# First attention of a decoder layer: rotated queries, scores over 64 rows, the mask as a TensorE product

## The chip, the core and the metric

The kernel runs on one core of one Trainium2 chip. The metric is the device time of one execution in microseconds. Three timed runs of the kernel before gave 1333.85, 1334.43 and 1336.25 us, so its median is 1334.43 us.

## The reference, cut to what matters

The program is one pre-norm decoder layer on x of shape (16, 128, 256): `x += attn(ln(x))`, `x += xattn(ln(x), ctx)`, `x += ffn(ln(x))`. Only the first attention is changed. It has 16 query heads, 4 key heads, a head size of 128 and a window of 64:

```python
q, k = rope((x @ Wq).heads(16)), rope((x @ Wk).heads(4))   # t * cos + rotate_half(t) * sin
v = (x @ Wv).heads(4)
s1 = q[..., :64] @ k[..., :64].T / 8                       # two score maps for each head
s2 = q[..., 64:] @ k[..., 64:].T / 8
s1, s2 = where(allowed, s1, -1e30), where(allowed, s2, -1e30)
a1, a2 = softmax(s1), softmax(s2)
d = relu(a1 - lam * a2);  d = d / (d.sum(-1) + 1e-6)
out = (d @ v).merge() @ Wo
```

`rotate_half` exchanges the two halves of 64 features, with a minus on one of them. So a rotated query needs, for each row, a value that stands 64 rows away.

## The kernel before, in words

One program, with instructions put by hand on five in-order queues: TensorE (PE), VectorE (DVE), ScalarE (ACT), GpSimd (POOL) and SyncE (SP, which issues the DMAs). Semaphores join them. Three stages follow one another: first attention (to about 500 us), cross attention (to about 890 us), the feed-forward part with its experts.

In the first attention the outer loop runs over 4 groups of heads (one key head and its 4 query heads), and in each group over 16 units `u`, one per sequence of the batch. So there are 64 units, n = 16g + u. Four units make a chunk; j = u mod 4 is the place in it. Features stand on the 128 partitions, tokens on the free axis. While the units of one chunk are worked on, the projections of the next chunk are made beside them: six items, k, q0 to q3 and v, each over 4 x 128 tokens. `A_SLOT` (L288) says at which place (j, slot) each item is made; slot 0 is at the beginning of a unit, slot 1 behind the transposes. `A_ITEMS` (L286) is their order. All go through one PSUM bank (PJ), so TensorE starts an item only when the one before has been taken out of the bank (`a_pf` for k and q, `a_vf` for v).

What the engines do for a unit, each in its own order (`a_unit` of each engine):

- TensorE: slot 0; the scores of unit n (L669); transposes of the weights of unit n-2 (L683, L685), which wait for POOL's norm; slot 1; the product with v (L692), which waits for ACT's copy `pt`; the output projection of unit n-3 (L701). Slot items are L553 (k, q) and L608 (v).
- DVE: denominator and its reciprocal for n-2 (L1100, L1105); the addition to x (L1110); `rec` and `ratio` for n-1 (L1080, L1084), which wait for the exponentials of n-1; the take of the slot 0 item (`a_take`); `rho` (L1088); `oal` (L1140); the difference of the two maps of n-1 (`a_diff`, L1094, 4 instructions); the maxima of the scores of n (L1148, L1149); the take of the slot 1 item.
- ACT: slot 0 (v is taken by ACT); the copy `pt` for n-2; the clipping of unit n-1 (L1500, 4 times with its sum), which waits for DVE's difference; the 8 exponentials of unit n (L1456), which wait for the maxima; the copy `oah`; and last the mask (L1511), copied into the two PSUM banks that the scores of unit n+2 will add onto.
- POOL: the norm of unit n-2 (L1687, 2 instructions) behind `rden`; the addition that finishes the rotated key (`a_keys`, L1681); at some units low parts of weights.

The rotation before is asymmetric. The key is rotated in full: DVE writes k\*cos and the crossed k\*sin into `ktmp` (3 instructions), POOL adds them, and SP copies the result with 4 DMAs into `kva`, so that map m has its 64 key rows twice (L462 to L465). The query is not rotated: DVE writes two products of it with tables (`qab`, L1054), and the score product contracts over 128 rows, which adds up both terms of the rotation. A score product takes 64 queries (stationary) against 128 or 64 keys; heads of odd and even number go to the upper and lower 64 PSUM partitions.

The start differs: the first chunk's items go through four banks (`turns` = 4), and the two first units put the mask under the scores by a product of the identity with `maskb` (L665).

Of the kernel before, what the change touches and what calls it, by code (L numbers as in the profile page):

```python
# [106 lines left out]
def decoder_kernel(nc, x, ctx_in, in_wqk, in_wv, in_wo, in_lam, in_taba, in_rawb, in_tabb, in_kvtab,  # L107
# [11 lines left out]
    with ctx:  # L119
# [129 lines left out]
        a_kd, a_tn = sem("a_k_copied"), sem("a_table_negated")  # L249
        a_sc, a_mx, a_ex = sem("a_scores"), sem("a_negmax"), sem("a_exp")  # L250
        a_mk = sem("a_mask_in_place")
# [34 lines left out]
        A_ITEMS = ["k", "q0", "q1", "q2", "v", "q3"]  # L286
        AN, AV = len(A_ITEMS), A_ITEMS.index("v")
        A_SLOT = {(0, 1): 0, (1, 0): 1, (1, 1): 2, (2, 1): 3, (3, 0): 4, (3, 1): 5}  # L288
# [152 lines left out]
        def _(sp):  # L441
            for c in range(NC):
# [6 lines left out]
                if c == 1:  # L449
                    sp.dma_start(taba[:, :, :], in_taba).then_inc(a_tab, 16)  # L450
# [6 lines left out]
            for g in range(NG):  # L457
                if g < NG - 1:
                    sp.wait_ge(a_lo, g * AW + AW)
                    sp.dma_start(raw_a[:, :, :], in_wqk[g + 1]).then_inc(a_raw, 16)  # L460
                for c in range(NC):
                    sp.wait_ge(a_k, g * NC + c + 1)  # L462
                    for m in range(2):
                        for at in (0, 64):
                            sp.dma_start(kva[at:at + 64, c % 2, m, :], ktmp[64 * m:64 * m + 64, 0, :]).then_inc(a_kd, 16)  # L465
# [81 lines left out]
        def _(pe):  # L547
# [69 lines left out]
            def a_unit(g, u, first=False, final=False, drain=False):  # L617
# [286 lines left out]
            pe.wait_ge(a_vf, 1)  # L904
            pe.wait_ge(s_cst, 3)
# [81 lines left out]
        def _(dve):  # L987
# [47 lines left out]
            def a_take(g_to, c, item, turns=1):  # L1035
# [6 lines left out]
                if item == 0:  # L1042
                    wait(dve, a_kd, 64 * chunk)
# [916 lines left out]
```

## Time and profile before

| | before |
|---|---|
| median of 3 runs | 1334.43 us |
| profiled execution | 1336.08 us, its span 1334.2 us |
| TensorE busy | 1262.3 us (95%) |
| VectorE busy | 837.2 us (63%) |
| ScalarE busy | 720.2 us (54%) |
| GpSimd busy | 467.6 us (35%) |
| granted TensorE clock, mean | 0.986 |

The span is what the engines' records cover; the execution's own time is 1.9 us longer. PE counts a matmul from issue to its modelled end, and PEld, its weight load, runs beside it. A matmul in fp32 leaves two records, so the 16 score products of a unit show as x32. "Idle before" behind a row says how long the engine stood before the instruction and what released it. A line number can be that of a helper: ACT's copies all stand at L1423 and go by their tiles, `ps<-maskb` being the mask.

### The profile page before, as it was taken

What the parts mean: (1) busy time and instruction counts of PE and PEld (TensorE: products, weight loads), DVE (VectorE), ACT (ScalarE), POOL (GpSimd) and SP (SyncE); (2) the same over time, 40 slices, a digit from 0 to 9 for tenths busy, and PEclk for the clock granted to TensorE, in tenths of its full rate; (3) what the DMA queues carried; (4) which work ended last, traced back from release to release, by engine and by line L of the source; (5) the groups of instructions that cost most, each with busy time, mean ns of one, the idle gap of its engine ahead of it and who ended that gap; (6) DMA issues with size and microseconds to landing.
All of it is one profiled execution on the core that took longest, in us unless ns stands there. A gap on an engine that the chain in (4) does not pass through costs nothing.

```text
span 1334.2 us, 27286 instructions
## 1 busy us (share of the span) xinstructions
PE 1262.3 (95%) x9584; PEld 993.9 (74%) x9584; DVE 837.2 (63%) x1986; ACT 720.2 (54%) x2746; POOL 467.6 (35%) x451
## 2 busy tenths in 40 slices
PE   5799999999999787999999999989999999999998
PEld 4678888888887564666666666657888888888887
DVE  6788888888888676566666656775443443434433
ACT  2788888888887753444444444464232332423322
POOL 3122113212211124445444544641152353533532
PEclk9899999999999989999999999999899999999999
DMA  6002000200012101111202101200324341144340
GB/s 222 17 18 57 18 17 18 57 17 17 17 34 92 31 16 48 60 33 58 67 17 92 33 17 33 76 1 1 111 67 139 68 126 52 39 139 77 57 93 31
DMA packets 34737, 72.78 MB, mean 55 GB/s; under 512 B 7872, under 2 KB 12992, under 8 KB 33344
## 3 DMA queue, kind: packets, MB, share of 16 engines
q1 hardware_dynamic: 34624, 71.32, 20.2%
q8 instruction: 66, 1.08, 0.3%
q14 instruction: 47, 0.39, 0.1%
HBM read 52.29 MB, written 2.23 MB: 41 GB/s over the span
## 4 chain that ended last, share of the span: by engine, by line
PE 74%; DVE 9%; ACT 8%; issue 4%; POOL 2%; DMA 1%; SPq 1%; DVEq 0%; POOLq 0%; ACTq 0%
PE ps L553 33%; PE ps L945 9%; PE ps L669 5%; PE ps L701 4%; PE ps L738 3%; PE ps L832 3%; ACT ea L1456 3%; PE ps L692 3%; PE ps L842 2%; PE ps L814 2%; PE ps L822 2%; PE ps L608 2%; ACT ea L1500 2%; DVE ea L1094 1%; PE ps L683 1%
## 5 line engine op out<-in xcount | busy, mean ns | idle before, releaser
L1828 POOL TENSOR_TENSOR sg<-sg,cw 128x512 f32<-128x512 f32 x88 | 113.6, 1291 | 260.4 <-ACT sg L1619 257.0
L1397 DVE TENSOR_TENSOR hh<-ps,sg 128x512 f32<-128x512 f32 x100 | 69.1, 691 | 179.1 <-POOL sg L1828 161.4
L1423 ACT ACTIVATE hhh<-hh 128x512 fp32r<-128x512 f32 x100 | 63.2, 632 | 213.8 <-DVE hh L1397 211.6
L1456 ACT ACTIVATE ea<-ps,negmax 128x64 f32<-128x64 f32 (+1 forms) x512 | 165.1, 342 | 6.7 <-DVE negmax L1149 6.7
L1423 ACT ACTIVATE pt<-ps 128x512 f32<-128x512 f32 x128 | 77.1, 602 | 169.7 <-PE ps L822 112.2
L1196 DVE TENSOR_TENSOR qcs<-ps,tabb 128x512 f32<-128x512 f32 x192 | 123.5, 686 | 64.8 <-PE ps L553 64.4
L553 PE MATMUL ps<-xnh,wch 128*128 128x512 f32 x400 | 157.3, 393 | 0.0
L553 PE MATMUL ps<-xnl,wch 128*128 128x512 f32 x400 | 157.1, 393 | 0.0
L553 PE MATMUL ps<-xnh,wcl 128*128 128x512 f32 x400 | 155.7, 389 | 0.0
L1687 POOL TENSOR_TENSOR ea<-ea,rden 128x128 f32<-128x128 f32 (+1 forms) x128 | 62.2, 506 | 263.1 <-DVE rden L1105 263.1
L1694 POOL TENSOR_TENSOR eb<-eb,rsum 128x512 f32<-128x512 f32 x64 | 67.4, 1054 | 180.2 <-DVE rsum L1240 180.0
L945 PE MATMUL ps<-wch,hhh 128*128 128x256 f32 x400 | 115.8, 290 | 4.2 <-DVE hhl L1399 2.4
L1399 DVE TENSOR_TENSOR hhl<-hh,hhh 128x512 fp32r<-128x512 f32 x100 | 75.5, 755 | 69.8 <-ACT hhh L1423 69.8
L945 PE MATMUL ps<-wch,hhl 128*128 128x256 f32 x400 | 113.6, 284 | 0.0
L945 PE MATMUL ps<-wcl,hhh 128*128 128x256 f32 x400 | 113.6, 284 | 0.0
L1456 ACT ACTIVATION_READ_ACCUMULATOR ea<-ps,negmax 128x1 f32 x512 | 107.3, 210 | 0.0
L1456 ACT ACTIVATE eb<-ps,negmax 128x128 f32<-128x128 f32 x256 | 90.7, 369 | 26.0 <-DVE negmax L1234 25.7
L669 PEld LDWEIGHTS ps<-kva,qab 128*64 128x64 f32 x2048 | 93.8, 140 | 13.2 <-issue 8.1
L669 PE MATMUL ps<-kva,qab 128*64 128x128 f32 (+1 forms) x2048 | 103.0, 254 | 0.0
L1619 ACT ACTIVATE sg<-ps 128x512 f32<-128x512 f32 x100 | 59.8, 598 | 71.9 <-PE ps L553 71.2
L701 PE MATMUL ps<-woh,oah 128*128 128x256 f32 x256 | 97.5, 381 | 0.7 <-DVE oal L1140 0.7
L1054 DVE TENSOR_TENSOR qab<-ps,taba 128x512 f32<-128x512 f32 x128 | 82.1, 683 | 19.5 <-PE ps L553 19.0
(154 smaller groups left out, 3307.3 us busy)
## 6 DMA issues: line engine op xcount, KB each, us to landing
raw_w<-in_rawb_dram SPq DMA_DIRECT2D x4, 2432.0 KB, 8.9
kva<-ktmp SPq DMA_DIRECT2D x64, 128.0 KB, 2.3
kvt<-qcs SPq DMA_DIRECT2D x64, 128.0 KB, 2.3
cw<-comb_d SPq DMA_DIRECT2D x32, 256.0 KB, 5.0
raw_w<-in_rawc_dram SPq DMA_DIRECT2D x4, 1920.0 KB, 8.4
cw<-comb_d SPq DMA_DIRECT2D x16, 224.0 KB, 4.8
raw_a<-in_wqk_dram SPq DMA_DIRECT2D x4, 768.0 KB, 5.8
cw<-comb_d SPq DMA_DIRECT2D x16, 192.0 KB, 5.8
```

The source lines that it names most:

```text
L553: last = pe.matmul(out_ap, w, m, start=n == 0, stop=n == len(steps) - 1)
L669: last = pe.matmul(to[rows, h // 2, :], qab[:, c % 2, m, h, S * j + at:S * j + at + QH], kva[:, c % 2, m, S * j:S * j + keys], start=False ...
L701: last = pe.matmul(ps[:, YB, 0:DM], o_[:, (u - 3) % 2, h, :], w_[:, h, :], start=h == 0 and i == 0, stop=h == HG - 1 and i == 2)
L945: last = pe.matmul(ps[:, j // 2, DM * (j % 2):DM * (j % 2 + 1)], h_[:, par, S * j:S * (j + 1)], w_[:, t, 2 * KT * 128:RC_T], start=begin a ...
L1054: last = dve.tensor_tensor(quads(dst), src, bcast(taba[:, tab, :]), ALU.mult)
L1196: last = dve.tensor_tensor(quads(qcs[:, b_at(t), m, :]), quads(bk), bcast(tabb[:, b_table(t), m, :]), ALU.mult)
L1397: dve.tensor_tensor(hh[:, par, :], bank(C_U[par]), sg[:, par, :], ALU.mult).then_inc(c_h, 1)
L1399: dve.tensor_tensor(hhl[:, par, :], hh[:, par, :], hhh[:, par, :].bitcast(f32), ALU.subtract)\
L1423: return act.activation(dst, src, ACT.Copy)
L1456: last = act.activation(dst(m, h), src, ACT.Exp, bias=negmax[:, par, i:i + 1], accum_out=sums[:, par, i:i + 1])
L1694: pool.tensor_tensor(src[:, par, :, :], src[:, par, :, :], rec[:, par, :].unsqueeze(2).broadcast_to([128, HG, S]), ALU.mult).then_inc(done, 1)
L1828: pool.tensor_tensor(sg[:, par, :], sg[:, par, :], cw[:, c % 2, t, :], ALU.mult).then_inc(c_hs, 1)
```

## The change

The query is now rotated too. DVE writes q\*cos into `qab[:, par, 0, h]` and q\*sin into `qab[:, par, 1, h]`; two DMAs for each head carry the latter, its halves exchanged, into the place of the other parity; POOL adds the two. The key goes from POOL's addition straight into `kva`, with no copy. Each score product contracts over the 64 rows of its own map, so the two maps use different halves of the array's rows, and the order alternates over the four quarters. The mask goes under the scores of every unit as two products of the identity with `maskb`, and ACT's copy of it is gone; the scores of unit n wait for the exponentials of unit n-2 instead. The items move to other slots, and v becomes the last.

```diff
-        A_ITEMS = ["k", "q0", "q1", "q2", "v", "q3"]
+        A_ITEMS = ["k", "q0", "q1", "q2", "q3", "v"]
-        A_SLOT = {(0, 1): 0, (1, 0): 1, (1, 1): 2, (2, 1): 3, (3, 0): 4, (3, 1): 5}
+        A_SLOT = {(0, 0): 0, (0, 1): 1, (1, 0): 2, (1, 1): 3, (2, 0): 4, (3, 0): 5}
...
@@ SP, for each chunk @@
-                    sp.wait_ge(a_k, g * NC + c + 1)
-                    for m in range(2):
-                        for at in (0, 64):
-                            sp.dma_start(kva[at:at + 64, c % 2, m, :], ktmp[64 * m:64 * m + 64, 0, :]).then_inc(a_kd, 16)
+                    for h in range(HG if g or c else 0):
+                        sp.wait_ge(a_pf, (g * NC + c) * AW + (h + 2))
+                        for to, at in ((64, 0), (0, 64)):
+                            sp.dma_start(qab[to:to + 64, 1 - c % 2, 1, h, :], qab[at:at + 64, c % 2, 1, h, :])\
+                              .then_inc(a_qx[h], 16)
@@ TensorE, a_unit @@
-                        pe.wait_ge(a_kd, 64 * (g * NC + (c + 1)))
-                    wait(pe, a_mk, n - 1)
+                        pe.wait_ge(a_k, g * NC + (c + 1))
+                        pe.wait_ge(a_qr, HG * (g * NC + (c + 1)))
+                    wait(pe, a_ex, n - 1)
                     for m in range(2):
-                        sc = A_S[u % 2][:, m, 0:SW]
-                        if first and u < 2:
-                            pe.matmul(sc, idb[:, :], maskb[:, :], start=True, stop=False, skip_group_check=True)
-                        for at, to, keys in ((QH, late(sc), S), (0, early(sc), QH)):
-                            for h in range(HG):
-                                rows = slice(QH * (h % 2), QH * (h % 2) + QH)
-                                last = pe.matmul(to[rows, h // 2, :],
-                                                 qab[:, c % 2, m, h, S * j + at:S * j + at + QH],
-                                                 kva[:, c % 2, m, S * j:S * j + keys],
-                                                 start=False, stop=at == 0, skip_group_check=True)
+                        pe.matmul(A_S[u % 2][:, m, 0:SW], idb[:, :], maskb[:, :], start=True, stop=False,
+                                  skip_group_check=True)
+                    for at, part, keys in ((QH, late, S), (0, early, QH)):
+                        for m, h in ((0, 0), (1, 1), (0, 1), (1, 0), (0, 2), (1, 3), (0, 3), (1, 2)):
+                            rows, d = slice(QH * (h % 2), QH * (h % 2) + QH), slice(64 * m, 64 * m + 64)
+                            last = pe.matmul(part(A_S[u % 2][:, m, 0:SW])[rows, h // 2, :],
+                                             qab[d, c % 2, 0, h, S * j + at:S * j + at + QH],
+                                             kva[d, c % 2, 0, S * j:S * j + keys],
+                                             start=False, stop=at == 0, skip_group_check=True)
@@ DVE, a_take, a query; the first chunk (turns > 1) crosses the sines by itself @@
+                dve.tensor_tensor(quads(qab[:, par, 0, h, :]), src, bcast(taba[:, 0, :]), ALU.mult)
+                if turns == 1:
+                    last = dve.tensor_tensor(quads(qab[:, par, 1, h, :]), src, bcast(taba[:, 1, :]), ALU.mult)
+                else:
+                    for to_, at in ((64, 0), (0, 64)):
+                        last = dve.tensor_tensor(...)      # 64 rows each
@@ ACT, a_unit @@
-                if not drain and not (final and u >= UN - 2):
-                    act.wait_ge(a_ex, n + 1)
-                    copy(A_S[u % 2][:, :, 0:SW], maskb[:, :].unsqueeze(1).broadcast_to([128, 2, SW])).then_inc(a_mk, 1)
@@ POOL @@
-                pool.tensor_tensor(ktmp[:, 0, :], ktmp[:, 0, :], ktmp[:, 1, :], ALU.add).then_inc(a_k, 1)
+                pool.tensor_tensor(kva[:, c % 2, 0, :], ktmp[:, 0, :], ktmp[:, 1, :], ALU.add).then_inc(a_k, 1)
+            def a_queries(g_to, c, heads):
+                for h in heads:
+                    ...
+                        pool.wait_ge(a_qx[h], 32 * (g_to * NC + c))
+                    q = qab[:, c % 2, 0, h, :]
+                    pool.tensor_tensor(q, q, qab[:, 1 - c % 2, 1, h, :], ALU.add).then_inc(a_qr, 1)
+            A_TURNED = [(), (0,), (1, 2), (3,)]
@@ POOL, a_unit, behind a_norm and a_keys @@
+                a_queries(g + 1 if c == NC - 1 else g, (c + 1) % NC, A_TURNED[j])
@@ POOL, before the first unit @@
             a_keys(0, 0)
             ln_low(1)
+            a_queries(0, 0, range(HG))
```

## Rows read from the trace of the kernel before

**Rows 1.** The page: busy time of each engine; the chain by engine.

```profile
PE 1262.3 (95%) x9584; PEld 993.9 (74%) x9584; DVE 837.2 (63%) x1986; ACT 720.2 (54%) x2746; POOL 467.6 (35%) x451
PE 74%; DVE 9%; ACT 8%; issue 4%; POOL 2%; DMA 1%; SPq 1%; DVEq 0%; POOLq 0%; ACTq 0%
```

**Rows 2.** Windows (us from:to, length, busy of each engine, granted clock, DMA share, GB/s).

```profile
62.50:405.50 343.00, 339.51 (x3157) 282.43 (x3156) 285.14 (x814) 296.51 (x1424) 78.55 (x133) 1.00 0.11 26
450.00:470.00 20.00, 11.49 (x102) 8.74 (x100) 12.49 (x42) 10.69 (x51) 2.96 (x5) 0.85 0.02 4
```

**Rows 3.** The chain of waits from 288 us (start, us, what).

```profile
292.33 1.49 PE ps L669 x32
...
294.38 1.38 PE ps L553 x6
...
298.05 1.79 PE ps L608 x16
```

**Rows 4.** Timeline of ScalarE (start, us, instruction, idle before it).

```profile
289.55 0.26 ACT L1500 ACTIVATE ea<-ea 128x64 f32<-128x64 f32 x1 [0.27 <-DVE ea L1094]
...
295.46 0.26 ACT L1500 ACTIVATE ea<-ea 128x64 f32<-128x64 f32 x1 [0.44 <-DVE ea L1094]
...
301.92 0.60 ACT L1423 ACTIVATE pt<-ps 128x512 f32<-128x512 f32 x1 [1.01 <-PE ps L685]
```

**Rows 5.** Timeline of VectorE over one unit and parts of its neighbours.

```profile
282.79 0.69 DVE L1044 TENSOR_TENSOR ktmp<-ps,taba 128x512 f32<-128x512 f32 x1 [0.17 <-PE ps L553]
283.50 1.39 DVE L1046 TENSOR_TENSOR ktmp<-ps,taba 64x512 f32<-64x512 f32 x2
...
285.87 0.41 DVE L1084 TENSOR_TENSOR ratio<-rec,sums 128x4 f32<-128x4 f32 x1
286.64 1.29 DVE L1054 TENSOR_TENSOR qab<-ps,taba 128x512 f32<-128x512 f32 x2 [0.35 <-PE ps L553]
287.85 0.15 DVE L1088 TENSOR_TENSOR rho<-ratio,a_gap 128x4 f32<-128x4 f32 x1
...
288.51 1.00 DVE L1094 SCALAR_TENSOR_TENSOR ea<-ea,rho 128x64 f32<-128x64 f32 x4
...
291.75 0.18 DVE L1105 RECIPROCAL rden<-den 128x4 f32<-128x4 f32 x1
...
293.33 0.18 DVE L1080 RECIPROCAL rec<-sums 128x4 f32<-128x4 f32 x1 [0.53 <-ACT ea L1456]
```

**Rows 6.** GpSimd: its timeline, and all key additions from 60 us (ns; starts).

```profile
284.97 1.30 POOL L1681 TENSOR_TENSOR ktmp<-ktmp 128x512 f32<-128x512 f32 x1 [5.36 <-DVE ktmp L1046]
...
292.01 0.97 POOL L1687 TENSOR_TENSOR ea<-ea,rden 128x128 f32<-128x128 f32 x2 [4.81 <-DVE rden L1105]
...
311.29 1.29 POOL L1681 TENSOR_TENSOR ktmp<-ktmp 128x512 f32<-128x512 f32 x1 [5.37 <-DVE ktmp L1046]
...
L1681 POOL TENSOR_TENSOR ktmp<-ktmp x14: 1264/1292/1297, 69.8 to 420.4; 128x512 f32<-128x512 f32 x14
```

**Rows 7.** Line L1084, duration min/median/max in ns.

```profile
L1084 DVE TENSOR_TENSOR ratio<-rec,sums x64: 161/163/449, 40.1 to 486.3; 128x4 f32<-128x4 f32 x64
```

**Rows 8.** Line L465: four issues of one chunk; time to landing.

```profile
259.19 2.54 SPq L465 DMA_DIRECT2D kva<-ktmp  x4
...
DMA to landing us min/median/max: 2.2/2.3/5.2
```

**Rows 9.** Weight loads of TensorE: the mask product and scores; cross attention's scores in quarters.

```profile
41.75 0.10 PEld L665 LDWEIGHTS ps<-maskb,idb 128*128 128x128 bf16 x1
42.02 0.75 PEld L669 LDWEIGHTS ps<-kva,qab 128*64 128x64 f32 x16 [0.17 <-issue]
...
523.87 0.43 PEld L814 LDWEIGHTS ps<-kt,qr 64*64 64x64 f32 x16 [0.35 <-issue]
```

**Rows 10.** The start: DVE's takes of q0 to q2; TensorE's first mask product.

```profile
20.70 4.03 DVE L1054 TENSOR_TENSOR qab<-ps,taba 128x512 f32<-128x512 f32 x6
...
29.14 0.32 PE L665 MATMUL ps<-maskb,idb 128*128 128x384 bf16 x1 [1.69 <-DVE qab L1054]
```

More of the change, by code:

```diff
@@ L248, in decoder_kernel @@
         a_pj, a_pf, a_k = sem("a_projected"), sem("a_projection_taken"), sem("a_k_ready")
-        a_kd, a_tn = sem("a_k_copied"), sem("a_table_negated")
+        a_qx = [sem(f"a_q_sines_crossed{h}") for h in range(HG)]
+        a_qr, a_tn = sem("a_q_rotated"), sem("a_table_negated")
         a_sc, a_mx, a_ex = sem("a_scores"), sem("a_negmax"), sem("a_exp")
-        a_mk = sem("a_mask_in_place")
         a_r2, a_rt, a_rh = sem("a_rec2"), sem("a_ratio"), sem("a_rho")
@@ L449, in _ @@
                 if c == 1:
-                    sp.dma_start(taba[:, :, :], in_taba).then_inc(a_tab, 16)
+                    sp.dma_start(taba[0:64, :, :], in_taba[0:64]).then_inc(a_tab, 16)
+                    sp.dma_start(taba[64:128, 0, :], in_taba[64:128, 1]).then_inc(a_tab, 16)
+                    sp.dma_start(taba[64:128, 1, :], in_taba[64:128, 0]).then_inc(a_tab, 16)
+                    sp.dma_start(taba[64:128, 2:6, :], in_taba[64:128, 2:6]).then_inc(a_tab, 16)
                     for at in (0, QH):
@@ L904, in _ @@
             pe.wait_ge(a_vf, 1)
+            pe.wait_ge(a_pf, AW)
             pe.wait_ge(s_cst, 3)
@@ L1042, in a_take @@
                 if item == 0:
-                    wait(dve, a_kd, 64 * chunk)
+                    wait(dve, a_k, chunk)
                     dve.tensor_tensor(quads(ktmp[:, 0, :]), src, bcast(taba[:, 4, :]), ALU.mult)
@@ L1051, in a_take @@
                 h = a_tile(item) - 1
-                to = ((qab[:, par, 0, h, :], 0), (qab[:, par, 1, h, :], 1))
-                for dst, tab in to:
-                    last = dve.tensor_tensor(quads(dst), src, bcast(taba[:, tab, :]), ALU.mult)
+                dve.tensor_tensor(quads(qab[:, par, 0, h, :]), src, bcast(taba[:, 0, :]), ALU.mult)
[3 more added lines that the diff above has]
+                    for to_, at in ((64, 0), (0, 64)):
+                        last = dve.tensor_tensor(quads(qab[to_:to_ + 64, 1 - par, 1, h, :]), src[at:at + 64],
+                                                 taba[at:at + 64, 1, :].unsqueeze(1).broadcast_to([64, CB, S]),
+                                                 ALU.mult)
                 last.then_inc(a_pf, 1)
@@ L1326, in _ @@
             ln_low(0)
-            dve.wait_ge(a_tab, 16)
+            dve.wait_ge(a_tab, 64)
             ln_norm(1)
@@ L1334, in _ @@
             dve.tensor_copy(late(maskb[:, :]), masku.unsqueeze(1).broadcast_to([128, XP, S])).then_inc(s_cst, 1)
-            dve.tensor_scalar(taba[64:128, 0, :], taba[64:128, 0, :], -1.0, None, ALU.mult).then_inc(a_tn, 1)
+            dve.tensor_scalar(taba[64:128, 1, :], taba[64:128, 1, :], -1.0, None, ALU.mult).then_inc(a_tn, 1)
             dve.tensor_scalar(taba[:, 3, :], taba[:, 3, :], -1.0, None, ALU.mult).then_inc(a_tn, 1)
@@ L1480, in slot @@
                             if r == 0:
-                                act.wait_ge(a_sc, NG * UN - CB)
+                                act.wait_ge(a_sc, NG * UN - CB + 1)
                             copy(kt2[:, CB * r:CB * (r + 1), :], quads(bank(PJ))).then_inc(b_kvc, 1)
@@ L1680, in a_keys @@
                 pool.wait_ge(a_pf, (g_to * NC + c) * AW + 1)
-                pool.tensor_tensor(ktmp[:, 0, :], ktmp[:, 0, :], ktmp[:, 1, :], ALU.add).then_inc(a_k, 1)
+                pool.tensor_tensor(kva[:, c % 2, 0, :], ktmp[:, 0, :], ktmp[:, 1, :], ALU.add).then_inc(a_k, 1)
+            def a_queries(g_to, c, heads):
+                for h in heads:
+                    if isinstance(g_to, int) and g_to == 0 and c == 0:
+                        pool.wait_ge(a_pf, h + 2)
+                    else:
+                        pool.wait_ge(a_qx[h], 32 * (g_to * NC + c))
+                    q = qab[:, c % 2, 0, h, :]
+                    pool.tensor_tensor(q, q, qab[:, 1 - c % 2, 1, h, :], ALU.add).then_inc(a_qr, 1)
+            A_TURNED = [(), (0,), (1, 2), (3,)]
             def a_norm(n, par):
@@ L1716, in a_unit @@
                     return
-                if final and c >= NC - 2:
-                    if u == UN - 2 * CB:
-                        a_keys(g, NC - 1)
+                if final and c == NC - 1:
                     return
@@ L1722, in a_unit @@
                     a_keys(g + 1 if c == NC - 1 else g, (c + 1) % NC)
+                a_queries(g + 1 if c == NC - 1 else g, (c + 1) % NC, A_TURNED[j])
+                if final:
+                    return
                 if 0 < u - CB * (NC - 2) <= CB:
```

## Prediction

> **What bounds the kernel now.** I read the page first: TensorE is busy for 95% of the span and holds 74% of the chain that ended last [rows 1]. Then the windows: from 62.5 to 405.5 us, where only attention units run, TensorE is busy for 339.5 of 343.0 us, ScalarE for 296.5, VectorE for 285.1, at full clock [rows 2]. That reads like a kernel bound by TensorE, for which cheaper scores would be a gain. But a busy share includes modelled ends and says nothing of which wait ends last, so I went through one chunk in the timelines.
>
> There a second limit shows. Clipping starts at 289.55 and again at 295.46, 5.91 us apart, and the second start was released by VectorE's difference, with ScalarE idle for 0.44 us before it [rows 4]. This is a loop with no slack, since both queues are in order: ScalarE clips unit n-1 and then makes the exponentials of unit n; only when these are done does VectorE start `rec` (293.33, idle 0.53 before it, released by ScalarE [rows 5]), then ratio, whatever item is taken in slot 0, `rho`, `oal`, the difference; and this releases the next clipping. ScalarE's part is 289.55 to 293.33, 3.8 us; VectorE's part to 295.46 is 2.1 us. A take in slot 1 lies beside ScalarE's 3.8 us and costs nothing; a take in slot 0 lengthens the loop by its full time. Before, only q0 is taken in slot 0: 286.64 to 287.85, 1.2 us, behind 0.35 us of waiting for TensorE [rows 5].
>
> The chunk takes 311.29 - 284.97 = 26.3 us, from one key addition to the next [rows 6]. TensorE's own work in it: a unit with one item is 292.33 to 298.05, 5.72 us, four of them 22.9; one more item 1.38 and v 1.79 [rows 3] make 26.1. The loop is 4 x 5.91 + 1.2 = 24.8, and where TensorE is late in it, it waits: 1.0 us for the transposes in the unit of v [rows 4], 0.35 at q0 [rows 5], together the other 1.4. So TensorE sets the pace, with the loop only 1.5 us a chunk below.
>
> **The change part by part.**
>
> *Scores.* The chain gives 1.49 us a unit to the 32 score records [rows 3]. Not shown before is their form in quarters with full masks. The nearest row: cross attention's 16 records of 64x64 in 0.43 us, against 0.75 for 16 records of the present form [rows 9]. The new unit has 32 records with 1.5 times the columns of those 16: 0.43 x 1.5 = 0.65 us if columns count, 0.43 x 2 = 0.86 if records do. The two mask products cost 0.27 each from load to load (41.75 to 42.02 [rows 9]), 0.54 together. Sum 1.2 to 1.4, and up to 0.3 more for the changes of form between mask, scores and transposes: -0.3 to +0.2 us a unit. I take -0.15, or -0.6 us a chunk of TensorE's time. It can only pay down to the loop, 1.5 us below.
>
> A rule speaks against more. The Trainium skill, "TensorEngine Tiling (Array Packing)", Key Properties, says that a change of the tiling mode drains TensorE; each unit gets one more such change. The same page, Instruction Overhead, gives about 60 cycles to each matmul whatever its size; from this, as an estimate, 32 records cost 0.8 us at 2.4 GHz, which agrees with the larger of the two figures from the row. By both the saving would be about nothing.
>
> *Mask off ScalarE.* The copy lay behind `oah` and before `pt`, and ScalarE still stood idle for 0.44 us before the difference came [rows 4]. Worth 0 in units bound by the loop, at most the 1.0 us in v's unit if TensorE were late there, which the moved slots make rare. The new wait for the exponentials of unit n-2 is over a unit earlier: 0.
>
> *Slots.* Now k is taken in (0,0), q1 in (1,0), q3 in (2,0); q0 and q2 in slots 1; v on ScalarE. The take of k has three instructions, 282.79 to 284.89 = 2.1 us [rows 5]. So the loop carries 2.1 + 1.2 + 1.2 where it carried 1.2: 4 x 5.91 + 4.5 = 28.1 us a chunk. TensorE's own work, 26.1 - 0.6 = 25.5, stays under it and is no longer the bound. Net +1.8 us a chunk, with nothing else. An item on TensorE waits for the take of the one before it; q0's, in unit j = 0, comes only behind k's take, and its own take is then due behind difference and maxima, about 2.8 us on, against 1.4 us of projection: hidden.
>
> *Additions on POOL.* Five of 1.29 us a chunk instead of one [rows 6]; POOL has room (78.6 of 343 us busy [rows 2]). What they cost is a port. `ratio`, with two inputs from SBUF, takes 0.163 us at the median but up to 0.449 [rows 7]; the one at 285.87 took 0.41 and ended when the key addition did (284.97 + 1.30) [rows 5, 6]. `ratio`, `rho` and the difference are such instructions, and all stand in the loop. By place:
> - j = 0: the key addition starts 0.08 behind k's take and runs 1.3; the difference is due 0.7 behind it (`rho` to difference, 287.85 to 288.51 [rows 5]): +0.6.
> - j = 1: q0's halves land about 3.0 us behind its take (0.6 an issue, 2.3 to landing [rows 8]); the addition runs from 3.0 to 4.3. `rho` is due some 3.4 behind that take: +0.9, or +0.5 if `rho` passes first and the difference waits.
> - j = 2: POOL's norm starts 0.26 behind `rden` and takes 0.97 [rows 5, 6], then q1's addition follows at once, to 2.5 behind `rden`; `ratio` is due 1.8 behind it: +0.7; then q2's addition meets `rho`: +0.2.
> - j = 3: q3's addition is over before `ratio`: 0.
>
> That is 2.4 if all fall so, 0 if none does. I take 2.0. The Trainium skill, "SBUF — State Buffer", section "SBUF: two separate sides", calls this pair of ports an exclusive lock, held for a whole instruction, against VectorE operations with two SBUF inputs; the 0.41 us agrees, and by the rule all of 2.4 would be paid.
>
> *Crossing by DMA.* Eight DMAs a chunk on SP instead of four; 8 x 0.6 = 4.8 us of issue in a chunk. Behind them stands only the next group's weight load, due a group later. q3, the last, is taken at j = 2, and its sum is needed at the next j = 0, some 13 us on, against 3.0 + 1.3 and a norm: hidden.
>
> *Start.* Four heads have a third instruction in DVE's take: 4 x 0.67 = 2.7 us (4.03 / 6 each [rows 10]), and POOL adds the last after that, 1.3: the first scores (29.14 [rows 10]) come 3 to 4 us later. But k's take of the next chunk fills that gap. +1 for it, and +2 for the other units of the first chunk. The last chunk with takes (from 405 us) is stretched by layer-norm work on VectorE: +4, as elsewhere.
>
> **Sum.** New chunk 28.1 + 2.0 = 30.1 against 26.3: +3.8. From 69.8 to 420.4 us there are 13 chunks [rows 6] (27.0 each; the loop's branches and weight splits are in both): 13 x 3.8 = 49.4. With 3 and 4: +56. The profiled execution took 1336.1 us (span 1334.2), 1.7 above the median of the runs: 1336.1 + 56 = 1392.1, less 1.7 gives **1390.5 us**, which I round to 1391. The last four units and the other stages: 0.
>
> **The rivals.**
>
> *A. The takes matter, the port doesn't.* Additions fall between VectorE's reads: 13 x 1.8 = 23.4, + 5 = +28: 1363 us. For it: `ratio` was free at its median before [rows 7]. Against: five times as many additions of 1.29 us. Chance 0.20.
>
> *B. TensorE sets the beat (faster).* If VectorE's slot 0 takes weren't on the last path, TensorE's score block would decide in every unit. The place is the score block, its price -0.3 us in each of 64 units, -19, and 3 to 4 us back at the start: 1319 us. It decides if the loop stays under 26.3 us a chunk, that is if slot 0 carries under 2.7 us. For it: 339.5 of 343 us busy [rows 2]. Against: the 4.5 us of slot 0. Chance 0.12.
>
> *C. The clock falls as well.* TensorE would stand idle in each unit. From 450 to 470 us, busy for 11.5 of 20 us, it was granted 0.85 of the clock [rows 2], so some stretches at 1.2 GHz instead of 2.4. 25.5 us of work a chunk at 0.85 are 30.0, just under 30.1; at 0.8 they are 31.9: +1.8 a chunk, 13 x 1.8 = +23: 1414 us. Against: in my drawing no idle stretch of TensorE is over 1.5 us. Chance 0.12.
>
> *D. Nothing moves,* gains and losses level: 0.04.
>
> **How the numbers follow.** The forecast has 0.52. Slower are it, A and C: 0.84; faster B: 0.12; same (within 0.2%, 2.7 us, about what can be told here) 0.04. The range leaves out B and D, 16 in 100, and little else: from 1345, where A is with half its excess, to 1418, where C is with a little more.
>
> **What would show it.** Right: clipping starts about 8.6, 8.0, 8.1 and 5.9 us apart in a chunk; key additions 30 us apart; VectorE waits less and for ScalarE alone; TensorE's idle before slot items released by VectorE (`ktmp`, `qab`); `ratio`, `rho` or the difference with maxima near 1.3 us; scores plus mask 1.2 to 1.5 us. Wrong: key additions under 27 us apart, or TensorE still without idle time.

## The result, and the profile after

The changed kernel takes 1403.51 us at the median of four runs (1401.55 to 1405.54), against 1334.30 us of the kernel before on the same chip: a ratio of 1.0513 [1.05, 1.0526], slower by 69 us. The profiled execution took 1401.55 us, its span 1399.7 us. The forecast of 1391 us had the sign and most of the size (+57 us of the +69), and the range held the time.

The page of the kernel after (busy time of each engine, and the chain by engine), against [rows 1]:

```profile
PE 1264.5 (90%) x9708; PEld 957.9 (68%) x9708; DVE 869.2 (62%) x1990; ACT 678.1 (48%) x2684; POOL 549.4 (39%) x515
PE 56%; DVE 18%; ACT 15%; issue 7%; POOL 2%; DMA 1%; SPq 0%; DVEq 0%; POOLq 0%; ACTq 0%
```

TensorE works as long as before (1264.5 us against 1262.3) and its share of the chain that ended last falls from 74% to 56%; VectorE's and ScalarE's double. The same stretch of attention as in [rows 2], in the view of windows:

```profile
62.50:405.50 343.00, 294.87 (x2779) 217.33 (x2778) 263.85 (x686) 221.86 (x1157) 122.18 (x156) 0.98 0.17 40
```

TensorE now stands idle for 48 of 343 us where it was idle for 3.5. The granted clock of the stretch is 0.98, where it was 1.00. Every engine but GpSimd is less busy (on ScalarE in part because the mask's copy is gone), and none of them is full: that points to a loop of waits, not to an engine that has too much to do. The view of waits from 80 to 420 us names its links (engine, what waited <- who released it: us in total, times, longest):

```profile
ACT ea L1510 <- DVE ea L1104: 72.6, 38, 3.3
DVE rec L1090 <- ACT ea L1466: 52.3, 41, 1.9
PEld ps L557 <- DVE qab L1059: 14.5, 23, 1.1
PEld ps L557 <- DVE ktmp L1051: 11.8, 11, 1.7
```

ScalarE's clip waits for VectorE's difference, VectorE's `rec` waits for ScalarE's exponentials, and TensorE waits until VectorE has taken an item. In the same view of the kernel before, the first two waits were short:

```profile
DVE rec L1080 <- ACT ea L1456: 19.9, 36, 1.1
ACT ea L1500 <- DVE ea L1094: 11.3, 29, 0.7
```

Lines moved by about ten: the clip is L1510 (before L1500), the difference L1104, `ratio` L1094, `rho` L1098, the query's take L1057 and L1059, the key's addition L1688, the query's L1698, the norm L1706.

Timeline of ScalarE, the clips of one chunk, as [rows 4] (start, us, instruction, idle before it):

```profile
388.92 0.26 ACT L1510 ACTIVATE ea<-ea 128x64 f32<-128x64 f32 x1 [3.02 <-DVE ea L1104]
396.78 0.26 ACT L1510 ACTIVATE ea<-ea 128x64 f32<-128x64 f32 x1 [1.70 <-DVE ea L1104]
404.62 0.26 ACT L1510 ACTIVATE ea<-ea 128x64 f32<-128x64 f32 x1 [1.67 <-DVE ea L1104]
410.53 0.26 ACT L1510 ACTIVATE ea<-ea 128x64 f32<-128x64 f32 x1
418.91 0.26 ACT L1510 ACTIVATE ea<-ea 128x64 f32<-128x64 f32 x1 [2.08 <-DVE ea L1104]
```

The distances are 7.86, 7.84, 5.91 and 8.38 us, for units j = 1, 2, 3 and 0: one chunk in 30.0 us. The key's additions stand 29.99 us apart (386.79 and 416.78 below), where 30 was predicted. Only j = 3, which takes nothing in slot 0 and meets no addition, keeps the bare loop of 5.91 us. GpSimd and VectorE over the same chunk, against [rows 6] and [rows 5]:

```profile
386.79 1.29 POOL L1688 TENSOR_TENSOR kva<-ktmp 128x512 f32<-128x512 f32 x1 [3.72 <-DVE ktmp L1051]
393.94 1.28 POOL L1698 TENSOR_TENSOR qab<-qab 128x512 f32<-128x512 f32 x1 [1.59 <-DMA qab<-qab]
399.23 0.97 POOL L1706 TENSOR_TENSOR ea<-ea,rden 128x128 f32<-128x128 f32 x2 [4.02 <-DVE rden L1115]
400.16 1.28 POOL L1698 TENSOR_TENSOR qab<-qab 128x512 f32<-128x512 f32 x1
401.79 1.27 POOL L1698 TENSOR_TENSOR qab<-qab 128x512 f32<-128x512 f32 x1 [0.35 <-DMA qab<-qab]
416.78 1.30 POOL L1688 TENSOR_TENSOR kva<-ktmp 128x512 f32<-128x512 f32 x1 [3.61 <-DVE ktmp L1051]
```

```profile
384.61 0.69 DVE L1049 TENSOR_TENSOR ktmp<-ps,taba 128x512 f32<-128x512 f32 x1
385.31 1.39 DVE L1051 TENSOR_TENSOR ktmp<-ps,taba 64x512 f32<-64x512 f32 x2
387.54 1.34 DVE L1104 SCALAR_TENSOR_TENSOR ea<-ea,rho 128x64 f32<-128x64 f32 x4
394.21 1.02 DVE L1098 TENSOR_TENSOR rho<-ratio,a_gap 128x4 f32<-128x4 f32 x1
400.77 0.69 DVE L1094 TENSOR_TENSOR ratio<-rec,sums 128x4 f32<-128x4 f32 x1
402.58 0.49 DVE L1098 TENSOR_TENSOR rho<-ratio,a_gap 128x4 f32<-128x4 f32 x1
403.60 0.99 DVE L1104 SCALAR_TENSOR_TENSOR ea<-ea,rho 128x64 f32<-128x64 f32 x4
```

Lay them side by side by their ends. GpSimd's addition at 393.94 ends at 395.22, and so does `rho` (394.21 + 1.02), an instruction over 128 x 4 numbers. The addition at 400.16 ends at 401.44, `ratio` at 401.46. The one at 401.79 ends at 403.06, `rho` at 403.07. The key's ends at 388.08 and costs the difference that it meets 0.35 us (1.34 against 0.99 at 403.60). In the median nothing of this is seen, as `ratio` shows (the view of one line, min/median/max ns; [rows 7] before):

```profile
L1094 DVE TENSOR_TENSOR ratio<-rec,sums x64: 161/163/775, 41.6 to 550.4; 128x4 f32<-128x4 f32 x64
```

TensorE's block of mask and scores, in the timeline of its weight loads, against [rows 3, 9]:

```profile
400.44 0.12 PEld L668 LDWEIGHTS ps<-maskb,idb 128*128 128x128 bf16 x2 [0.27 <-issue]
400.87 0.76 PEld L673 LDWEIGHTS ps<-kva,qab 64*64 64x64 f32 x32 [0.32 <-issue]
401.70 0.14 PEld L687 LDWEIGHTS ps<-idf,ea 128*64 128x64 f32 x2
```

From 400.44 to 401.70 are 1.26 us, where the block had 1.49. TensorE's part did get cheaper, but with the new slots TensorE no longer sets the pace, so little could be gained by it.

**Where the 69 us are.** Clip starts of all 64 units, read from the two traces, before and after (us):

| | before | after | more |
|---|---|---|---|
| fourth clip (first chunk done) | 66.8 | 77.1 | +10.3 |
| the next 52 units (13 chunks) | 347.6 | 402.7 | +55.1 |
| the 4 units after them (last chunk with takes) | 34.4 | 33.9 | -0.5 |
| the last 4 | 39.9 | 39.1 | -0.8 |
| last clip | 488.7 | 552.8 | +64.1 |

The other stages add 1.4 us, which makes the 65.5 us between the two spans.

### The profile page after: what moved, and what is told of

Same layout as the page of the kernel before. It is cut to its first block, busy times and chain, and to the rows that moved or that the text cites. A ratio compares the mean times of both kernels' runs of the same rounds, so it can differ in the third digit from the quotient of the medians.

```text
span 1399.7 us, 27606 instructions
## 1 busy us (share of the span) xinstructions
PE 1264.5 (90%) x9708; PEld 957.9 (68%) x9708; DVE 869.2 (62%) x1990; ACT 678.1 (48%) x2684; POOL 549.4 (39%) x515
## 4 chain that ended last, share of the span: by engine, by line
PE 56%; DVE 18%; ACT 15%; issue 7%; POOL 2%; DMA 1%; SPq 0%; DVEq 0%; POOLq 0%; ACTq 0%
PE ps L557 27%; PE ps L950 9%; ACT ea L1466 8%; DVE ea L1104 4%; ACT ea L1510 4%; PE ps L742 3%; PE ps L836 3%; PE ps L846 2%; PE ps L818 2%; PE ps L826 2%; PE ps L705 2%; DVE ktmp L1051 1%; DVE qab L1059 1%; DVE rho L1098 1%; PE ps L696 1%
## 5 line engine op out<-in xcount | busy, mean ns | idle before, releaser
L1433 ACT ACTIVATE pt<-ps 128x512 f32<-128x512 f32 x128 | 77.1, 602 | 193.7 <-PE ps L826 112.4
L1706 POOL TENSOR_TENSOR ea<-ea,rden 128x128 f32<-128x128 f32 (+1 forms) x128 | 62.3, 508 | 237.8 <-DVE rden L1115 237.8
L1510 ACT ACTIVATE ea<-ea 128x64 f32<-128x64 f32 (+1 forms) x256 | 69.3, 274 | 97.4 <-DVE ea L1104 97.2
L1466 ACT ACTIVATE eb<-ps,negmax 128x128 f32<-128x128 f32 x256 | 90.7, 369 | 25.8 <-DVE negmax L1244 25.5
L557 PE MATMUL ps<-xnh,wah 128*128 128x512 f32 x160 | 71.8, 449 | 34.0 <-DVE qab L1059 17.4
L696 PE MATMUL ps<-pt,kva 128*128 128x512 f32 x128 | 71.4, 640 | 33.8 <-DVE oal L1150 20.8
```

The source lines that it names most:

```text
L557: last = pe.matmul(out_ap, w, m, start=n == 0, stop=n == len(steps) - 1)
L696: pe.matmul(bank(OB), quads(kva[:, (w // CB) % 2, 2, :])[:, w % CB, :], pt[:, u % 2, :, :], start=True, stop=True).then_inc(a_pv, 1)
L1433: return act.activation(dst, src, ACT.Copy)
L1466: last = act.activation(dst(m, h), src, ACT.Exp, bias=negmax[:, par, i:i + 1], accum_out=sums[:, par, i:i + 1])
L1510: last = act.activation(e, e, ACT.Relu, accum_out=rsum[:, par, h:h + 1])
```

## The experiments

Ten more kernels were run. A beat is the distance from one unit's clip to the next. Beats are given in the order j = 1, 2, 3, 0, for one plain chunk, the fifth of the table's row of 13, in which GpSimd makes no low parts of weights and no group ends (before: 7.74, 5.90, 6.93, 5.90; after: 7.90, 7.89, 5.91, 8.48). "A chunk" is the time of the 13 chunks over 13 (before 26.74, after 30.98).

### Slots alone

```diff
 (the kernel before)
-        A_ITEMS = ["k", "q0", "q1", "q2", "v", "q3"]
-        A_SLOT = {(0, 1): 0, (1, 0): 1, (1, 1): 2, (2, 1): 3, (3, 0): 4, (3, 1): 5}
+        A_ITEMS = ["k", "q0", "q1", "q2", "q3", "v"]
+        A_SLOT = {(0, 0): 0, (0, 1): 1, (1, 0): 2, (1, 1): 3, (2, 0): 4, (3, 0): 5}
... (and TensorE waits once, before the first unit, until the k and q items of the first chunk are taken)
```

> The kernel before with the new places of the items alone (k in (0,0), q1 in (1,0), q3 in (2,0), v last); rotation, scores and mask as before. Loop theory (VectorE's takes in slot 0 lengthen the loop exponentials - ratio - take - difference - clipping): 4 x 5.91 + 2.1 + 1.2 + 1.2 = 28.1 us a chunk against 26.3 before, so +1.8 x 13 = +23, and 0 to 6 more at the start: 1355 to 1365 us. Port theory alone (only the additions on POOL cost): no change, 1334. TensorE theory (its work sets the pace): no change, 1334.

Measured: 1377.42 us, ratio 1.031 [1.0288, 1.0333]; a chunk 29.31 (+2.57), the first chunk +5.7. Beats 7.00, 6.99, 6.60, 8.54. ScalarE's clips in its timeline:

```profile
198.27 0.26 ACT L1501 ACTIVATE ea<-ea 128x64 f32<-128x64 f32 x1 [0.51 <-DVE ea L1095]
205.26 0.26 ACT L1501 ACTIVATE ea<-ea 128x64 f32<-128x64 f32 x1 [0.36 <-DVE ea L1095]
...
220.40 0.26 ACT L1501 ACTIVATE ea<-ea 128x64 f32<-128x64 f32 x1 [1.76 <-DVE ea L1095]
```

A query in slot 0 makes a beat of 7.0 us, 1.1 over the bare loop; the key, with the collision of its addition, 8.5. This is the loop as predicted, without any rotation of queries and with scores as before. The time is 12 us above the range expected. Two things are seen in a plain chunk: the key's addition already meets the difference here (1.34 us), and in v's unit TensorE, with its dearer score block, is 0.7 us late. So the new places alone cost 43 us with the old score block.

### Small additions

The query additions work on 8 of the 512 columns, so all takes, DMAs and waits stay, and most of the rotation is left out.

```diff
-                    pool.tensor_tensor(q, q, qab[:, 1 - c % 2, 1, h, :], ALU.add).then_inc(a_qr, 1)
+                    pool.tensor_tensor(q[:, 0:8], q[:, 0:8], qab[:, 1 - c % 2, 1, h, 0:8], ALU.add).then_inc(a_qr, 1)
```

> The changed kernel, with POOL's additions for the queries made on 8 columns instead of 512; it leaves out most of the query's rotation. All semaphores, DMAs and waits stay. In the changed kernel's steady chunk the excess over a free port is about 0.86 (rho) + 0.53 (ratio) + 0.35 (rho) = 1.7 us behind these additions. Loop and port theory: -1.7 x 13 = -22, and -3 to -6 in the first chunk: 1374 to 1380 us, chunk 28.4 + loop branches. If the additions cost nothing: 1403. If all of the loss were the additions: 1340.

Measured: 1370.74 us, 1.0275 [1.025, 1.0301]; a chunk 28.88, beats 7.00, 7.00, 5.90, 8.48. The time is 3 us under the range expected. `ratio` never grows:

```profile
L1094 DVE TENSOR_TENSOR ratio<-rec,sums x64: 161/163/178, 41.7 to 517.3; 128x4 f32<-128x4 f32 x64
```

The length of the four additions is worth 33 us, 2.1 a chunk and 5.8 in the first chunk. j = 1 and 2 fall by 0.90 and 0.89 us, the price predicted for the port (0.9 each); the key's addition is whole here and still has its price. The crossing DMAs and the new waits, all still here, cost nothing that shows: rival A, the takes alone, would have been about this time.

### Takes spread

```diff
 (the kernel after)
-        A_SLOT = {(0, 0): 0, (0, 1): 1, (1, 0): 2, (1, 1): 3, (2, 0): 4, (3, 0): 5}
+        A_SLOT = {(0, 1): 0, (1, 0): 1, (1, 1): 2, (2, 0): 3, (2, 1): 4, (3, 0): 5}
-            A_TURNED = [(), (0,), (1, 2), (3,)]
+            A_TURNED = [(), (), (0, 1), (2, 3)]
```

> The changed kernel with items at (0,1) k, (1,0) q0, (1,1) q1, (2,0) q2, (2,1) q3, (3,0) v; POOL adds q0, q1 in unit 2 and q2, q3 in unit 3. The slot 0 takes are q0 and q2, 2.4 us instead of 4.5. Loop theory: 26.0 us a chunk and about 2 of port: 28.0 against 30.1, -2.1 x 13 = -27: 1372 to 1380 us. If k's place doesn't matter: 1403.

Measured: 1377.02 us, 1.031 [1.0292, 1.0329]. The key goes to slot 1, behind the maxima, and the beats become 7.64, 7.87, 7.12, 5.90: the one of j = 0 falls from 8.48 to 5.90. But v's unit, j = 3, goes from 5.90 to 7.12 though it takes nothing in slot 0: the additions of q2 and q3 now fall into it (`ratio` 0.69 us, the difference 1.69), so of the 2.6 us that j = 0 gives back, 1.2 are paid to the port again. The time is within what was expected.

### The mask back on ScalarE

```diff
 (the kernel after)
-                    for m in range(2):
+                    for m in range(2 if first and u < 2 else 0):
                         pe.matmul(A_S[u % 2][:, m, 0:SW], idb[:, :], maskb[:, :], start=True, stop=False, ...)
 (TensorE's scores wait for this copy again; ScalarE, as before the change)
+                    copy(A_S[u % 2][:, :, 0:SW], maskb[:, :].unsqueeze(1).broadcast_to([128, 2, SW])).then_inc(a_mk, 1)
```

> The changed kernel with the mask copied by ScalarE as before (undoes that part). Loop theory: neither TensorE nor ScalarE's place behind the exponentials is on the last path, so within 5 us of 1403. TensorE theory: the two mask products, 0.4 to 0.5 us in each of 62 units, come off: 1375. ScalarE theory (the copy costs 0.85 us a unit): 1440 or more.

Measured: 1404.44 us, 1.0527 [1.0509, 1.0545], the same as after within the intervals, as expected. Who puts the mask there is of no account while neither TensorE nor this place of ScalarE's queue is on the loop.

### The mask product alone

```diff
 (the kernel before)
-                        if first and u < 2:
+                        if True:
                             pe.matmul(sc, idb[:, :], maskb[:, :], start=True, stop=False, skip_group_check=True)
 (and ScalarE's copy of the mask is gone; the scores wait for the exponentials of unit n-2 instead)
```

> The kernel before with the mask put under the scores by two TensorE products in every unit, and ScalarE's copy gone; slots, rotation and scores as before. TensorE sets the pace there (26.1 us of work in a chunk of 26.3), and two products cost 0.4 to 0.54 us a unit: +1.6 to +2.2 a chunk, about 15 chunks: 1358 to 1367 us. Rival (ScalarE's 0.85 us a unit were what mattered): 1300 to 1334.

Measured: 1362.34 us, 1.0205 [1.0188, 1.0222], as expected; a chunk 28.74. Here TensorE sets the pace, and it pays in full: 2.0 us a chunk, 0.5 a unit, near the 0.54 of two products worked out in the prediction. In the view of windows it has no idle time left:

```profile
62.50:405.50 343.00, 342.27 (x3030) 274.59 (x3030) 269.69 (x756) 240.80 (x1271) 72.45 (x122) 1.00 0.10 25
```

### The quarters alone

The kernel before, with the loop over quarters of 64 rows and nothing else. One of the two terms of each rotated score is left out.

```diff
 (the kernel before; the loops become those of the kernel after)
-                                                 qab[:, c % 2, m, h, S * j + at:S * j + at + QH],
-                                                 kva[:, c % 2, m, S * j:S * j + keys],
+                                             qab[d, c % 2, m, h, S * j + at:S * j + at + QH],
+                                             kva[d, c % 2, m, S * j:S * j + keys],
```

> The kernel before with each score product contracting over 64 rows in quarters; it leaves out one of the two terms of the query's rotation, so no query is rotated, and nothing is added on POOL or SP. Score records 1.49 -> 0.8 us a unit, so TensorE's work falls to 23.3 us a chunk, under the loop of 24.8 + 0.25: a chunk of 25.1 to 25.4, -1.0 x 13 to -1.2 x 15: 1314 to 1321 us. If TensorE alone set the pace: 1334 - 0.7 x 64 = 1290. If the scores were no bound at all: 1334.

Measured: 1323.24 us, 0.9907 [0.9888, 0.9925]. This is what cheaper scores can bring when nothing is paid for them: 12 us; the time is 2 us above the range expected. The beats are 7.56, 5.91, 6.12, 5.90, together 25.5 where the kernel before has 26.5 (as a mean of the 13 chunks 26.2 against 26.7), and TensorE is no longer full (window 62.5 to 405.5):

```profile
62.50:405.50 343.00, 324.25 (x3241) 253.80 (x3234) 289.12 (x834) 301.75 (x1444) 78.89 (x134) 1.00 0.11 26
```

The loop, 4 x 5.91 + 1.2 = 24.8, stands right behind, as the prediction had it.

### Additions before the norm, in two forms

If the port is the cost, the additions belong where VectorE's long takes or its waits stand, not behind the norm. In the first form they wait for the difference that VectorE makes in the same unit (`a_df` at n, the difference of unit n-1):

```diff
 (the kernel after, GpSimd's a_unit; the calls behind the norm are gone)
+                if not drain and not (final and c == NC - 1):
+                    if j:
+                        wait(pool, a_df, n)
+                    if j == 1:
+                        a_keys(g + 1 if c == NC - 1 else g, (c + 1) % NC)
+                    a_queries(g + 1 if c == NC - 1 else g, (c + 1) % NC, A_TURNED[j])
                 if not (first and u < 2):
                     a_norm(n - 2, u % 2)
```

> The changed kernel with POOL's additions moved ahead of the norm of their unit, behind a wait for VectorE's difference; the key's addition goes to unit j = 1. VectorE reads nothing in pairs from SBUF for some 3.6 us from there. Port theory: rho, ratio and the difference are free again in 12 of 16 units of a group, 28.1 + 0.2 a chunk against 30.1, -1.8 x 13 = -23, and 3 to 5 less in the first chunk: 1373 to 1380 us. If the additions cost by their number and not by when they fall: 1403.

The second puts this together with the spread takes and the mask on ScalarE:

> Three cures together on the changed kernel: takes spread as in e3 (slot 0 carries q0 and q2), additions early as in e9, mask on ScalarE. Loop 4 x 5.91 + 2.2 = 25.8 us a chunk, TensorE 23.5: -4.3 x 13 = -56 from 1403, and 3 to 5 less at the start: 1342 to 1350 us. If it equals the kernel before in its steady chunks (26.3), the rest over 1334 is the first chunk. Rival (TensorE's waits for the one bank of the items bind): 1360.

Measured: 1600.83 us, 1.1988 [1.1968, 1.2008], and 1594.34 us, 1.1943 [1.1923, 1.1963]. Both came out more than 200 us above what was expected. Three rows of the first kernel, GpSimd's timeline and VectorE's:

```profile
289.68 1.26 POOL L1698 TENSOR_TENSOR qab<-qab 128x512 f32<-128x512 f32 x1 [8.97 <-DVE ea L1104]
290.90 0.96 POOL L1706 TENSOR_TENSOR ea<-ea,rden 128x128 f32<-128x128 f32 x2
```

```profile
283.74 0.18 DVE L1115 RECIPROCAL rden<-den 128x4 f32<-128x4 f32 x1
```

The norm could have started at 283.9, behind `rden`; it stood in the queue behind an addition that waited for the difference made later in the same unit (288.61 to 289.60), and started at 290.9, 7 us late. TensorE's transposes wait for the norm, and its queue holds slot 1, the product with v and the next scores behind them (its waits, 80 to 420 us):

```profile
PEld ps L687 <- POOL ea L1706: 99.5, 23, 5.9
```

What was written as a change of place on GpSimd made a loop through four engines. The beats were 12.2, 13.7, 10.7 and 8.1 us, and only j = 0, where GpSimd makes no addition and has no such wait, stays near its old length. TensorE was granted less of its clock too (a window from 75 to 660 us, all in the attention units, against 1.00 and 0.98 from 62.5 to 405.5 us before and after):

```profile
75.00:660.00 585.00, 399.96 (x3262) 301.56 (x3261) 279.69 (x815) 262.94 (x1384) 141.15 (x185) 0.83 0.11 27
```

How much of the loss is the clock's wasn't separated. These two runs say nothing of the port.

### Additions in VectorE's gap

The first form above with the wait on the difference that VectorE made in the unit before (`a_df` at n-1), which is done when the unit begins; the key's sum at j = 1, q0 and q1 at j = 2, q2 and q3 at j = 3.

```diff
 (against the first form; now also only where j > 0)
-                        wait(pool, a_df, n)
+                        wait(pool, a_df, n - 1)
-            A_TURNED = [(), (0,), (1, 2), (3,)]
+            A_TURNED = [(), (), (0, 1), (2, 3)]
```

> The cure of e9 done rightly: the wait is for the difference made in the unit before (a_df of n-1), which is over 2.4 us before rden, so the norm isn't held; key's sum in unit 1, q0 and q1 in unit 2, q2 and q3 in unit 3, two additions (2.6 us) at most in a gap of 3.6 us. Port theory: rho, ratio and the difference are free in most units; 28.1 to 28.3 us a chunk against 30.1, -1.8 x 13 = -23, 3 to 5 less in the first chunk: 1373 to 1381 us. If e9 lost its time to the additions' early place itself and not to the norm behind the wait: over 1403.

Measured: 1367.28 us, 1.0244 [1.0227, 1.0261], 36 us under the kernel after, with the same instructions and full additions. Beats 6.98, 6.99, 5.90, 8.13. GpSimd's timeline:

```profile
196.13 2.54 POOL L1698 TENSOR_TENSOR qab<-qab 128x512 f32<-128x512 f32 x2 [3.69 <-DVE ea L1104]
198.98 0.97 POOL L1706 TENSOR_TENSOR ea<-ea,rden 128x128 f32<-128x128 f32 x2 [0.31 <-DVE rden L1115]
```

VectorE beside them:

```profile
194.97 0.99 DVE L1104 SCALAR_TENSOR_TENSOR ea<-ea,rho 128x64 f32<-128x64 f32 x4
...
196.82 0.68 DVE L1057 TENSOR_TENSOR qab<-ps,taba 128x512 f32<-128x512 f32 x1
197.42 0.68 DVE L1059 TENSOR_TENSOR qab<-ps,taba 128x512 f32<-128x512 f32 x1
198.02 0.67 DVE L1110 SCALAR_TENSOR_TENSOR den<-sums,rsum 128x4 f32<-128x4 f32 x1
...
199.99 0.16 DVE L1094 TENSOR_TENSOR ratio<-rec,sums 128x4 f32<-128x4 f32 x1
```

Two additions start when the difference is done and run beside the maxima and a take, which read PSUM. What they meet is `den` (0.67 us, 0.16 without), which stands outside the loop: `rec` waited 0.57 for ScalarE all the same. The beats of j = 1 and 2 are those of the kernel with additions of 8 columns: the collision, not the addition, was the cost. That the places of the additions don't explain the loss of the two runs above is seen by the second of them, which has its query additions at the same j as here. The time came out 6 us below the expectation; the key's addition, moved as well, gives 0.35 a chunk of it (8.13 against 8.48).

### The three together

```diff
 (the kernel after, with)
  A_SLOT and A_TURNED: the key to (0, 1), q0 (1, 0), q1 (1, 1), q2 (2, 0), q3 (2, 1), v (3, 0)
  GpSimd: key and q0 before the norm at j = 2, q1 and q2 before it at j = 3, q3 behind it at j = 3
  the mask copied by ScalarE; all additions before the norm wait as in the run before this one
```

> e11's additions (key and q0 in unit 2, q1 and q2 in unit 3, q3 behind the norm of unit 3), takes spread as in e3, mask on ScalarE. Loop 24.8 + 1.1 = 25.9, + 0.9 where q3's addition meets ratio: 26.8 us a chunk, -3.3 x 13 = -43, and 3 to 5 less at the start: 1352 to 1360 us; above the kernel before, which e6 says can gain 12 us at most from cheaper scores. If TensorE's waits for the items' bank bind instead: 1375.

Measured: 1346.94 us, 1.0091 [1.0073, 1.0109]; a chunk 27.33, beats 7.55, 6.98, 6.12, 5.89, the first chunk +3.2. 57 us of the 69 are back (the time is 5 us under the range expected), and it is still 12 us slower than the kernel before. The quarters alone show a gain of 12 us at most; what is left on the other side is two query takes in slot 0 where before had one, and the first chunk (+3.2). The beat of j = 1 is 7.55 and not 7.0, close to what it is in the other kernels that take the key in slot 1 of j = 0 and q0 in slot 0 of j = 1 (before 7.74, takes spread 7.64, quarters alone 7.56): no addition falls there, but `ratio` took 0.46 us beside GpSimd's norm, and VectorE waited 0.21 us for q0. Of the complete versions none beats the kernel before (quarters alone leaves out a term), and no other was tried.

## Why the prediction came out as it did

**What bounds the kernel.** Right. The loop ScalarE, VectorE, ScalarE of 5.91 us shows in every kernel at the units that carry nothing: 5.90 or 5.91 in after, small additions, takes spread and quarters alone. It was put at 1.5 us a chunk below TensorE; cheaper scores alone brought 1.0 in a plain chunk. The busy shares don't show it. One sign didn't come as forecast: VectorE was to wait less, and its `rec` waits for ScalarE grew from 19.9 to 52.3 us (80 to 420 us).

**Slots.** Right in mechanism and, for a plain chunk, in size. Predicted 28.1 us a chunk without the port; the kernel with small additions has 28.4 in its plain chunk (7.00 + 7.00 + 5.90 + 8.48), of which 0.35 are the key's collision, and 28.88 as a mean. The key's take in slot 0 was predicted at 8.6 with the port's 0.6 in it; 8.38 to 8.48 was measured.

**Additions on POOL.** Right, and the step that I had least grounds for, since one row of 0.41 us carried it. Predicted for j = 0 to 3: 0.6, 0.9, 0.9, 0. Measured: 0.35, 0.86, 0.87, 0 (excess of the stretched instructions in the rows above). That is 2.08 a plain chunk against the 2.0 that I took. The query additions have 1.73 of it, and the plain chunks with and without their length differ by 1.8 (30.17 against 28.38); over all 13 chunks the difference is 2.10. The two kernels that prove it from opposite sides are the one with small additions (33 us back) and the one with full additions in the gap (36 us back). So 30.1 was right for the plain chunks (30.17 in the one of the beats, 30.0 above), and the term that was short is the rest: the sum set a plain new chunk of 30.1 against a plain old one of 26.3, and the means are 30.98 and 26.74. Read from the clips, the three chunks in which GpSimd also makes low parts of weights (in 3 of 16 units) take 31.4, 33.2 and 31.5 us, where before they took 27.0, and the three at a change of group 31.1 to 31.5, where before they took 26.1 to 26.4. So 13 x 3.8 = 49.4 became 55.1. With small additions these six are longer than the plain ones too (28.9 to 29.4 against 28.4), so the length of the query additions is only a part of it, and the rest stays open.

**Scores.** Taken at -0.15 us a unit, measured -0.23 (1.26 against 1.49, each from the block's first weight load to that of the transposes). The 32 records in quarters take 0.76 us, between the 0.65 by columns and the 0.86 by records. The estimate from the Trainium skill, "TensorEngine Tiling (Array Packing)", section Instruction Overhead, was 0.8 us, and the trace agrees; but the conclusion drawn beside it, that by both rules the saving would be about nothing, didn't hold: from the mask's first load to the first score's, with the change of form between, are 0.43 us (400.44 to 400.87), under the 0.54 taken for the two products alone.

**Mask off ScalarE, crossing by DMA.** Nothing, as predicted: 1404.4 us with the mask on ScalarE, and the small additions keep all DMAs without a loss of their own. Alone, in the kernel that TensorE bounds, the mask product is a loss of about 27 us. The part that looked like a relief was one only because another part had moved the bound.

**Start.** This is the term that was most mis-sized: +3 was taken, +10.3 measured. The first scores came 3.7 us later (32.89 against 29.14), as forecast, but this wasn't made good. The first chunk in the timeline of VectorE and GpSimd:

```profile
52.98 3.00 DVE L1104 SCALAR_TENSOR_TENSOR ea<-ea,rho 128x64 f32<-128x64 f32 x4
```

```profile
52.88 2.49 POOL L1698 TENSOR_TENSOR qab<-qab 128x512 f32<-128x512 f32 x2
```

Two additions back to back hold the difference for 2.0 us in place of 0.35, since in this chunk GpSimd is late and makes its additions close together; with small additions the fourth clip comes at 71.3 and not 77.1, so 5.8 of the 10.3 go with their length. Of the rest, the slots alone would make 5.7 and the small additions left 4.5, so the parts don't add up, and how they share isn't settled. One piece is seen: TensorE's weight loads stood 5.6 us before a transposition of the layer norm, into the bank that ScalarE had just finished reading v from.

```profile
61.74 0.71 PEld L564 LDWEIGHTS ps<-idf,xnt 128*128 128x128 f32 x4 [5.59 <-issue]
```

```profile
61.04 0.63 ACT L1433 ACTIVATE kva<-ps 128x512 f32<-128x512 f32 x1
```

That v's copy released it is read from the two times and was not tried. It has a second part: the granted clock fell to the lower level, 1.2 GHz, at 61.2 us, when TensorE had stood idle for some 5 us, and was at it for about 10 us. The windows from 60 to 70 us, before and after:

```profile
60.00:70.00 10.00, 10.00 (x81) 8.13 (x80) 9.05 (x23) 9.24 (x50) 1.21 (x3) 1.00 0.00 0
60.00:70.00 10.00, 7.54 (x51) 5.29 (x52) 4.33 (x12) 6.75 (x29) 1.04 (x3) 0.56 0.01 2
```

The block of mask and scores took 2.27 us there (62.65 to 64.92), where the next one, at full clock, took 1.26 (72.64 to 73.90). Between the third and the fourth clip, which lie at 66.5 and 77.1, 4.7 us of the 10.3 arise. With small additions the same window was granted 0.89. How much of the start's loss is the clock's wasn't separated. The +4 taken for the last chunk with takes didn't come (-0.5); why its long units swallow them wasn't tried. Between the profiled executions the forecast was +56 and the result +65.5: 7.3 too few in the first chunk, 5.7 in the thirteen, 4.5 too many in the last, 0.6 too few elsewhere, and the rest rounding. That the last took back a third of what the others lacked is luck. The other 3 of the 12.5 us are the medians' distance from the two profiled executions.

**The rivals.** *A* (takes matter, port not) is refuted by the 33 and 36 us. *B* (TensorE sets the beat) is refuted by TensorE's 48 us of idle time and by the mask on ScalarE, which takes two products a unit off TensorE and changes nothing. Quarters alone come near B's 1319 us with 1323, but not by its mechanism: there is no mask product, and of the four beats of a plain chunk the loop sets two (5.91 and 5.90). *C* (the clock) didn't happen in the thirteen chunks, with 0.98 in a window that has 48 us of idle time; it did happen for 10 us in the first chunk.

## What to carry to other kernels

- When TensorE is 99% busy, look for the loop of waits that stands right below it, and add up each queue's part of it. A cheaper matmul is worth only the distance to that loop (here 12 us in all), and a take put into the loop costs its full length in every round.
- A long GpSimd addition beside VectorE is priced by what it meets, not by its length: 2.1 us a chunk in their places behind the norm, nothing on the loop in the gap behind the difference. Look at the longest durations, and set the ends of the two engines' instructions side by side.
- Before moving an instruction ahead of another on an in-order queue, ask what it waits for and when in the same round that is made. A wait for something made in the same unit, where what was made in the unit before would do, cost over 200 us (1601 against 1367 us).

## What the runs showed of the hardware

- A VectorE instruction of 128 x 4 numbers with two inputs in SBUF, 0.16 us alone, took 1.02 us beside a GpSimd addition of 1.28 us, and its end fell on the addition's within 0.02 us. Four such instructions (0.99 us) took 3.00 beside two additions (2.49). The Trainium skill, "SBUF — State Buffer", section "SBUF: two separate sides", describes the shared ports as an exclusive lock that keeps a VectorE instruction with two SBUF inputs out while a GpSimd instruction holds them. The trace agrees in the main, and shows that the price is the overlap less 0.14 to 0.19 us: the key's addition of 1.29 us overlaps the difference for 0.54 and cost it 0.35, the one that met `rho` overlaps it for 1.01 and cost 0.86.
- VectorE's takes, which read PSUM and a table, lost nothing: 0.68 us each at 196.82 and 197.42, wholly beside two GpSimd additions, and 0.69 at 384.61 with GpSimd idle.
- The granted clock was 0.98 in a window of the kernel after with TensorE idle for 14% of it, 0.56 from 60 to 70 us in its first chunk, where it fell when TensorE had stood idle for some 5 us, and 0.83 over the units of the kernel whose beats were 8 to 14 us, with TensorE busy for 400 of 585 us. So rival C has a place, though not in the thirteen chunks of this change.
